# Causal attention on one core: row maxima from K = 32 row strips, two heads per reduction, and four score banks with one exponential for two heads

## The chip, the cores and the metric

The kernel runs on one core of one Trainium2 chip. The metric is the device time of one execution in microseconds (us), and the median of the runs is compared. Three runs of the kernel before gave 3187.44, 3190.36 and 3196.83 us.

## The reference

One transformer layer over T = 2048 tokens with D = 1024 features, in fp32: normalisation, causal attention with 32 query heads of 32 features in 8 groups of 4 (each group shares one key and one value head), an output projection, a second normalisation, and a feed-forward part with int4 weights. Cut to what the change touches:

```
q = (xn @ Wq)  as (32 heads, T, 32);  k, v = (xn @ Wkv) as (8 groups, T, 32) each
scores = q @ k.T                          # causal: key > query is -inf
weights = softmax(scores / sqrt(32))      # exp(s - rowmax) / sum of them
ctx = weights @ v
x = x + layernorm(ctx @ Wo + bo)
x = x + layernorm(ffn(layernorm(x)))
```

## The kernel before, in words

The program is a row of stages, each in its own block: `project_qk`, `attend`, `project_context`, `gate_and_up`, `project_down`. Only `attend` is changed.

`attend` handles the 8 groups one after another. A product in near fp32 is made from fp16 parts: a head's query is stacked in 96 partitions as (high, low, high) and its key as (high, high, low), so one 96-row matmul gives three partial products at once. A 97th row carries the negated row maximum of the query and the constant 256 on the key side, so that the score matmul (`scores`, L464) yields scores from which the maximum is already subtracted, and ScalarE takes the exponential straight from PSUM (L576).

For a group there are 40 steps, (b, k): query block b of 512 queries, key tile k of 128 keys, `k < 4 * (b + 1)`. 28 steps are 512 queries wide; the last three key tiles of each block are 384, 256 and 128 wide, 4 steps each. In each step TensorE makes the scores of four heads (transposed: keys on the partitions), ScalarE takes the exponentials into a ring of five steps (`PROB`), and TensorE multiplies them by the values one step later (`products`, L479, four heads in four 32-column strips of the array, fp32 operands) and by a vector of ones (`sums`, L493), after GpSimd has added two steps' exponentials together where it can (`add_pair`, L695).

The maxima of group g + 1 are found while group g is worked on. `units` lists the pieces: a unit is one head, one tile of 128 queries and up to 1024 keys; there are 96 in a group, handed out over the steps before `TURN` (step 37) by `share` and placed between the scores, products and sums by `cut`. TensorE makes a unit with one or two 96-row matmuls (L445) and, on the diagonal, a masking matmul of 128 columns (L449); VectorE reduces it (L588):

```
S1 = ps("s1", [P, 2, UNIT])          # two slots of two banks: maxima
S2 = ps("s2", [P, 2, BANK])          # two banks: scores, one head each
free = SLOTS * g + (n - 1 if n else 0)   # unit n waits for the reduction of unit n - 2
```

So unit n + 1 is made in the other slot while unit n is reduced. At `TURN` the maxima are transposed (L455), scaled (L600) and stored as row 97 of the query stack by a DMA (L408). Group 0's units come in `ahead`, before the first group, one half of a value tile (12 matmuls of 256 columns, L506 to L508) after every fourth unit.

The order on each engine is fixed by the program; semaphores join the engines. SyncE loads group g + 2 (`load_group`, six DMAs, 1.9 MB, three buffers) at the start of group g. TensorE runs the body of a group as a hardware loop over groups 0 to 6 and a copy of it for group 7 (`bodies`). VectorE has group 0, a loop over 1 to 6, and group 7; ScalarE loops over all 8 groups, GpSimd over 1 to 7.

Of the kernel before, what the change touches and what calls it, by code (L numbers as in the profile page):

```python
# [295 lines left out]
def attend(nc, x_hi, x_lo, wv_hi, wv_lo, qk_hi, qk_lo, v_sb, ident, identb, causal, ones, c_hi, c_lo, sem):  # L296

# [16 lines left out]
    UNIT = 2 * BANK  # L314
    RING = 5
    exp_scale = float(HD) ** -0.5 / MS
    VC = wv_hi.shape[2]

# [3 lines left out]

    assert T == 2 * UNIT
    half = NT // 2
# [3 lines left out]
    EARLY = NT // 4  # L328
    PART = UNITS // (2 * (NT - EARLY))
    SLOTS = UNITS + 1  # L330

    width = [BANK - max(0, k - TPB * b) * P for b, k in steps]
    TURN = STEPS - 3
    share = [min(UNITS, -(-UNITS * sum(width[:s]) // sum(width[:TURN]))) for s in range(STEPS + 1)]
    units_in = [range(share[s], share[s + 1]) for s in range(STEPS)]

# [28 lines left out]
    loaded, max_stored, buffer_free = sem("c_loaded"), sem("c_max_stored"), sem("c_buffer_free")  # L365
# [7 lines left out]


    S2_FREE, PROB_FREE, SUM_FREE, C_FREE, CN_FREE = 2, SUMS, 1, 2, 2

    with ExitStack() as ctx:
        sb = lambda n, s, d=F32: ctx.enter_context(nc.sbuf_tensor("c_" + n, s, d))
        ps = lambda n, s, d=F32: ctx.enter_context(nc.psum_tensor("c_" + n, s, d))
        Q, K = sb("q", [STACK + 1, 3, REP, T], F16), sb("k", [STACK + 1, 3, T], F16)  # L380
        V = sb("v", [P, NT, HD])
        PROB = sb("prob", [P, RING * REP, BANK])
        MAXES, NEGMAX = sb("maxes", [P, NT * REP, 2]), sb("negmax", [P, P])
# [3 lines left out]
        S1 = ps("s1", [P, 2, UNIT])  # L387
        S2 = ps("s2", [P, 2, BANK])
# [6 lines left out]

        @block.sync
        def _(sp):
            def load_group(g, buf):
                qrows, krows = bass.ds(g * P, P), bass.ds(D + g * HD, HD)
                for row, (qs, ks) in enumerate(((qk_hi, qk_hi), (qk_lo, qk_hi), (qk_hi, qk_lo))):  # L400
                    part = slice(row * HD, (row + 1) * HD)
                    sp.dma_start(Q[part, buf], qs[qrows, :].rearrange("(h d) t -> d h t", d=HD)
                                 ).then_inc(loaded, 16)
                    sp.dma_start(K[part, buf], ks[krows, :]).then_inc(loaded, 16)
# [5 lines left out]
            load_group(0, 0)  # L410
            sp.wait_ge(loaded, 96)
            load_group(1, 1)
            store_maxima(0, 0)
            sp.wait_ge(loaded, 192)
            load_group(2, 2)
            store_maxima(1, 1)
            with sp.Fori(1, GROUPS - 2) as g:
                sp.wait_ge(loaded, 96 * g + 192)
                sp.sem_inc(buffer_free, 1)
                sp.wait_ge(scores_done, REP * STEPS * g)  # L420
                sp.sem_inc(buffer_free, 1)
                load_group(g + 2, (g + 2) % 3)
                store_maxima(g + 1, (g + 1) % 3)
            store_maxima(GROUPS - 1, (GROUPS - 1) % 3)

        def bodies(eng, body, ahead):

            ahead()
            with eng.Fori(0, GROUPS - 1) as g:
                body(g, True)  # L430
# [899 lines left out]
```

## Time and profile before

| | |
|---|---|
| median of 3 runs | 3190.36 us (3187.44 to 3196.83) |
| profiled execution, first to last instruction | 3191.3 us |
| `project_qk` | 0 to 256 us |
| `attend`, value tiles and units of group 0 | 256 to 371.2 us |
| `attend`, groups 0 to 6 | 371.2 to 1385.9 us |
| `attend`, group 7 (no units) | 1385.9 to 1507.4 us |
| `project_context` and the stages behind it | 1510 to 3191.3 us |

For the profiled execution no time of its own is listed beside its span; the span lies 0.9 us over the median of the runs. Stage limits are read from the first matmul of a line. In the profile, "busy" of a matmul includes the time in which its last columns leave the array, so that matmuls issued one behind another overlap in the record.

### The profile page before, as it was taken

How to read it: one execution, taken by the hardware profiler on the slowest of the kernel's cores; microseconds unless marked ns; L12 is line 12 of the kernel's file. 1: busy time of each engine (PE TensorE's matmuls, PEld its weight loads, DVE VectorE, ACT ScalarE, POOL GpSimd, SP SyncE). 2: the span in 40 equal slices, each digit the busy share in tenths (PEclk: the TensorE clock that was granted, in tenths of full speed). 3: DMA queues.
4: the chain of work that ended last, by engine and by line, in shares of the span. 5: the costliest groups of instructions: out<-in, count | busy, mean ns of one | idle time of the engine just before them, and what ended most of it. 6: DMA issues, size and time to landing. Idle time of an engine off the chain costs nothing. (4 is left out here: it accounts for less than half of the span.)

```text
span 3191.3 us, 47284 instructions
## 1 busy us (share of the span) xinstructions
PE 2983.2 (93%) x16984; PEld 1287.0 (40%) x16984; DVE 1297.3 (41%) x1707; ACT 946.7 (30%) x1734; POOL 951.0 (30%) x754
## 2 busy tenths in 40 slices
PE   7997798989899899988995999999999999999998
PEld 3444333333333333321443444444444444444443
DVE  5326775756656576620564223322233221000101
ACT  3110255656555565566111111111121111000000
POOL 0000165646455455656112222222222221000101
PEclk9999999999999999999997999999999999999999
DMA  4312101010110100000322111111111110331310
GB/s 157 101 50 60 26 1 27 1 27 1 26 23 5 27 1 2 1 2 14 122 95 70 43 39 43 43 43 39 39 45 44 39 38 24 109 112 62 123 62 26
DMA packets 143507, 144.62 MB, mean 45 GB/s; under 512 B 44272, under 2 KB 120560, under 8 KB 143344
## 3 DMA queue, kind: packets, MB, share of 16 engines
q1 hardware_dynamic: 143344, 142.39, 14.8%
q8 instruction: 110, 1.80, 0.2%
q14 instruction: 53, 0.43, 0.1%
HBM read 92.41 MB, written 49.81 MB: 45 GB/s over the span
## 5 line engine op out<-in xcount | busy, mean ns | idle before, releaser
L588 DVE TENSOR_REDUCE c_maxes<-c_s 128x1 f32<-128x1024 f32 (+7 forms) x768 | 675.0, 905 | 322.5 <-PE c_s L449 172.2
L576 ACT ACTIVATE c_prob<-c_s 128x512 f32<-128x512 f32 (+3 forms) x1280 | 637.8, 532 | 442.2 <-PE c_s L464 243.5
L695 POOL TENSOR_TENSOR c_prob<-c_prob 128x512 f32<-128x512 f32 (+1 forms) x480 | 581.5, 1242 | 431.7 <-ACT c_prob L576 430.2
L464 PE MATMUL c_s<-c_q,c_k 97*128 (+2 forms) x1280 | 415.9, 360 | 77.7 <-ACT c_prob L576 31.1
L445 PE MATMUL c_s<-c_k,c_q 96*128 (+2 forms) x1280 | 371.9, 359 | 34.5 <-DVE c_maxes L588 31.1
L479 PE MATMUL c_ctx<-c_prob,c_v 128*32 128x512 f32 (+3 forms) x2560 | 307.2, 552 | 0.0
L1096 DVE SCALAR_TENSOR_TENSOR e_h<-e_up,e_silu 128x512 f32<-128x512 f32 (+1 forms) x88 | 60.8, 691 | 579.8 <-PE e_up L1058 579.8
L1145 POOL TENSOR_TENSOR e_hl<-e_h,e_hh 128x512 f16<-128x512 f32 (+1 forms) x88 | 101.9, 1158 | 589.0 <-ACT e_hh L1119 589.0
L1056 PE MATMUL e_gp<-x_hi,e_w_hi 128*128 128x512 f16 (+1 forms) x704 | 267.9, 381 | 2.5 <-DVE e_w_lo L1086 2.5
L1057 PE MATMUL e_gp<-x_lo,e_w_hi 128*128 128x512 f16 (+1 forms) x704 | 267.6, 380 | 0.0
L1058 PE MATMUL e_gp<-x_hi,e_w_lo 128*128 128x512 f16 (+1 forms) x704 | 267.6, 380 | 0.0
L1056 PE MATMUL e_up<-x_hi,e_w_hi 128*128 128x512 f16 (+1 forms) x704 | 266.8, 379 | 0.0
L1057 PE MATMUL e_up<-x_lo,e_w_hi 128*128 128x512 f16 (+1 forms) x704 | 266.8, 379 | 0.0
L1058 PE MATMUL e_up<-x_hi,e_w_lo 128*128 128x512 f16 (+1 forms) x704 | 266.8, 379 | 0.0
L464 PEld LDWEIGHTS c_s<-c_q,c_k 97*128 (+1 forms) x1280 | 118.8, 99 | 320.4 <-issue 165.3
L445 PEld LDWEIGHTS c_s<-c_k,c_q 96*128 (+1 forms) x1280 | 103.1, 99 | 324.6 <-DVE c_maxes L588 143.6
L1226 PE MATMUL f_yp<-wd_hi,f_h_hi 128*128 128x512 f16 x704 | 210.4, 381 | 12.1 <-DMA f_h_lo<-h_lo 12.1
L1226 PE MATMUL f_yp<-wd_hi,f_h_lo 128*128 128x512 f16 x704 | 210.3, 380 | 0.0
L1226 PE MATMUL f_yp<-wd_lo,f_h_hi 128*128 128x512 f16 x704 | 210.3, 380 | 0.0
L1119 ACT ACTIVATE e_hh<-e_h 128x512 f16<-128x512 f32 (+1 forms) x88 | 55.4, 630 | 476.5 <-DVE e_h L1096 476.5
L74 DVE BATCH_NORM_STATS2 f_norm_stats<-f_yp 128x6 f32<-128x512 f32 x16 | 11.2, 699 | 424.6 <-PE f_yp L1226 424.6
L1264 POOL TENSOR_TENSOR f_z<-f_x,f_z 128x1024 f32<-128x1024 f32 x16 | 37.2, 2347 | 435.4 <-DVE f_z L87 435.4
(142 smaller groups left out, 3409.2 us busy)
## 6 DMA issues: line engine op xcount, KB each, us to landing
h_hi<-e_hh SPq DMA_DIRECT2D x84, 128.0 KB, 1.8
h_lo<-e_hl SPq DMA_DIRECT2D x84, 128.0 KB, 1.7
f_h_hi<-h_hi SPq DMA_DIRECT2D x7, 1344.0 KB, 8.5
f_h_lo<-h_lo SPq DMA_DIRECT2D x7, 1344.0 KB, 6.9
b_x<-L_attn_x SPq DMA_DIRECT2D x16, 512.0 KB, 6.6
c_q<-qk_hi SPq DMA_DIRECT2D x16, 512.0 KB, 6.6
d_x<-L_attn_x SPq DMA_DIRECT2D x16, 512.0 KB, 5.1
x_dram<-d_x SPq DMA_DIRECT2D x16, 512.0 KB, 2.6
```

What stands on the lines that cost most here:

```text
L445: last = nc.tensor.matmul(S1[:, slot, c:c + n_c], Q[0:STACK, buf, h, t * P:(t + 1) * P], K[0:STACK, buf, u * UNIT + c:u * UNIT + c + n_c], ...
L464: last = nc.tensor.matmul(S2[:, h % 2, j:BANK], K[:, buf, k * P:(k + 1) * P], Q[:, buf, h, b * BANK + j:(b + 1) * BANK], start=True, stop= ...
L479: last = nc.tensor.matmul(CTX[h * HD:(h + 1) * HD, j:BANK], V[:, k, :], PROB[:, REP * (s % RING) + h, j:BANK], start=(k == 0), stop=(k == ...
L576: nc.scalar.activation(PROB[:, REP * (s % RING) + h, j:BANK], S2[:, h % 2, j:BANK], ACT.Exp, scale=exp_scale).then_inc(exp_done, 1)
L588: nc.vector.tensor_reduce(MAXES[:, h * NT + t, u:u + 1], S1[:, n % 2, 0:end], AX.X, ALU.max).then_inc(maxed, 1)
L695: last = nc.gpsimd.tensor_tensor(one, one, two, ALU.add)
L1056: nc.tensor.matmul(o, wh, x2_hi[:, k, tok], start=(k == 0), stop=False)
L1057: nc.tensor.matmul(o, wh, x2_lo[:, k, tok], start=False, stop=False)
L1058: last = nc.tensor.matmul(o, wl, x2_hi[:, k, tok], start=False, stop=(k == KC - 1))
L1096: nc.vector.scalar_tensor_tensor(H[0:n, b % 2, :], UP_[0:n, b % 2, :], HS * in_scale, SILU[0:n, b % 2, :], ALU.mult, ALU.mult).then_inc(h_ ...
L1145: nc.gpsimd.tensor_tensor(HL[0:n, b % 2, :], H[0:n, b % 2, :], HH[0:n, b % 2, :], ALU.subtract).then_inc(lo_done, 1)
L1226: last = nc.tensor.matmul(YP[:, u, s, n:n + BANK], stat, w[:, c, n:n + BANK], start=(c == 0 and a == 1), stop=(c == CHUNKS - 1 and z == 1))
```

## The change

Inside `attend`:

- The maxima come from the high halves alone: `QH` and `KH` hold a group's four query heads in four strips of 32 partitions, and the key's high half four times. A unit is now two heads, one tile of 128 queries and at most 512 keys: two matmuls of 32 rows in two row strips, into the two banks of `S1`, then on the diagonal two masking matmuls of 128 columns, and one reduction of both banks into two columns of `MAXES`. There are 80 units in a group.
- `S1` is one slot: unit n waits for the reduction of unit n - 1.
- `S2` is four banks, one for each head of the group. Scores are made, waited for and exponentiated two heads at a time: 80 exponentials in a group in place of 160, each over two banks.
- Units are matched to steps (`in_step`): one key chunk in both pairs of heads, so two units, in 34 steps; two chunks, so four units, in steps 9, 10 and 11; none from step 37 on.
- The query and key stacks have two buffers. SyncE loads the stack of group g + 1 at the start of group g and the heads of group g + 2 (`load_heads`, five DMAs, 1.0 MB) behind it.
- TensorE, VectorE and SyncE run groups 0 and 1, a loop with two turns over two groups each, and groups 6 and 7 (`all_groups`). The loops of ScalarE and GpSimd stay.
- While group 0's maxima are made, half a value tile stands after each of the first 24 units.

```diff
-    units = [unit for h in range(REP) for a in range(half)
-             for unit in ((h, half + a, 0), (h, a, 0), (h, NT - 1 - a, 1))]
...
+    step_width = [BANK - max(0, k - TPB * b) * P for b, k in steps]
+    PAIR = 2
+    tiles = [(t, u) for t in range(NT) for u in range(t // TPB + 1)]
...
+    def unit_width(tile):
+        t, u = tile[:2]
+        return min(BANK, (t + 1) * P - u * BANK)
...
+    waiting = {w: [tile for tile in tiles if unit_width(tile) == w] for w in range(P, BANK + P, P)}
+    in_step = [[waiting[w].pop(0)] if s < TURN else [] for s, w in enumerate(step_width)]
+    narrow = [s for s in range(TPB, TURN) if step_width[s] < BANK]
+    for w in sorted(waiting, reverse=True):
+        for tile in waiting[w]:
+            in_step[next(s for s in narrow if step_width[s] == w and len(in_step[s]) == 1)].append(tile)
+    in_step = [[(t, u, pair) for pair in range(PAIR) for t, u in row] for row in in_step]
...
-        Q, K = sb("q", [STACK + 1, 3, REP, T], F16), sb("k", [STACK + 1, 3, T], F16)
+        Q, K = sb("q", [STACK + 1, 2, REP, T], F16), sb("k", [STACK + 1, 2, T], F16)
+        QH, KH = sb("qh", [P, 2, T], F16), sb("kh", [P, 2, T], F16)
...
-        S1 = ps("s1", [P, 2, UNIT])
-        S2 = ps("s2", [P, 2, BANK])
+        S1 = ps("s1", [P, PAIR, BANK])
+        S2 = ps("s2", [P, REP, BANK])
...
+        def all_groups(eng, body):
+            for parity in range(2):
+                body(0, parity)
+            with eng.Fori(1, GROUPS // 2 - 1) as i:
+                for parity in range(2):
+                    body(i, parity)
+            for parity in range(2):
+                body(GROUPS // 2 - 1, parity)
...
+            def load_heads(g, buf):
+                sp.dma_start(QH[:, buf, :], qk_hi[bass.ds(g * P, P), :]).then_inc(heads_loaded[buf], 16)
+                for h in range(REP):
+                    sp.dma_start(KH[h * HD:(h + 1) * HD, buf, :], qk_hi[bass.ds(D + g * HD, HD), :]
+                                 ).then_inc(heads_loaded[buf], 16)
...
+            def unit(g, buf, n):
+                t, u, pair = units[n]
+                w = unit_width(units[n])
+                diag = u == t // TPB
+                if not (is_first(g) and n == 0):
+                    pe.wait_ge(maxed, SLOTS * g + n)
+                for h in range(PAIR):
+                    rows = slice((PAIR * pair + h) * HD, (PAIR * pair + h + 1) * HD)
+                    last = nc.tensor.matmul(S1[:, h, 0:w], QH[rows, buf, t * P:(t + 1) * P],
+                                            KH[rows, buf, u * BANK:u * BANK + w], start=True, stop=not diag)
+                if diag:
+                    for h in range(PAIR):
+                        last = nc.tensor.matmul(S1[:, h, w - P:w], identb[:], causal[:], start=False, stop=True)
                 last.then_inc(unit_done, 1)
...
                 for s in range(STEPS):
-                    scores(g, s, (0,))
-                    some_units(s, 0)
-                    scores(g, s, (1,))
+                    ns = list(units_in[s]) if more else []
+                    scores(g, parity, s, 0)
                     if s:
                         products(g, s - 1)
-                    some_units(s, 1)
-                    scores(g, s, (2,))
-                    some_units(s, 2)
-                    scores(g, s, (3,))
+                    for n in ns[:len(ns) // PAIR]:
+                        unit(g + 1, 1 - parity, n)
+                    scores(g, parity, s, 1)
                     sums(g, s)
-                    some_units(s, 3)
+                    for n in ns[len(ns) // PAIR:]:
+                        unit(g + 1, 1 - parity, n)
...
+                    for pair in range(PAIR):
+                        h = PAIR * pair
+                        act.wait_ge(scores_done, PAIR * STEPS * g + PAIR * s + pair + 1)
+                        nc.scalar.activation(PROB[:, REP * (s % RING) + h:REP * (s % RING) + h + PAIR, j:BANK],
+                                             S2[:, h:h + PAIR, j:BANK], ACT.Exp, scale=exp_scale).then_inc(exp_done, 1)
...
                 dve.wait_ge(unit_done, SLOTS * g + n + 1)
-                nc.vector.tensor_reduce(MAXES[:, h * NT + t, u:u + 1], S1[:, n % 2, 0:end],
+                nc.vector.tensor_reduce(MAXES[:, PAIR * pair:PAIR * pair + PAIR, t, u], S1[:, :, 0:unit_width(units[n])],
                                         AX.X, ALU.max).then_inc(maxed, 1)
```

## Rows read from the trace of the kernel before

**Rows 1.** The page: the span, and each engine's busy time.
```profile
span 3191.3 us, 47284 instructions
PE 2983.2 (93%) x16984; PEld 1287.0 (40%) x16984; DVE 1297.3 (41%) x1707; ACT 946.7 (30%) x1734; POOL 951.0 (30%) x754
```

**Rows 2.** Busy time by stretch: group 0's units, group 0, group 6, group 7.
```profile
core 0: us, PE busy (x) PEld busy (x) DVE busy (x) ACT busy (x) POOL busy (x), PEclk, DMA share, GB/s
267.40:371.20 103.80, 72.24 (x514) 44.87 (x515) 83.03 (x98) 5.88 (x13) 0.61 (x1) 0.99 0.10 21
371.20:518.00 146.80, 136.09 (x970) 45.86 (x971) 91.69 (x111) 83.41 (x165) 78.24 (x67) 0.97 0.11 23
1245.80:1385.90 140.10, 135.66 (x969) 45.65 (x969) 92.34 (x113) 81.73 (x164) 79.81 (x68) 0.97 0.01 1
1385.90:1507.40 121.50, 105.54 (x748) 26.69 (x744) 10.05 (x17) 81.22 (x166) 79.05 (x70) 0.96 0.00 1
```

**Rows 3.** Groups of VectorE by form, groups 0 to 7 (371 to 1507 us).
```profile
L588 DVE TENSOR_REDUCE c_maxes<-c_s 128x1 f32<-128x1024 f32 x280 | 339.3, 1218 | 189.2 <-PE c_s L445 137.8 <-PE c_s L449 50.0
...
L588 DVE TENSOR_REDUCE c_maxes<-c_s 128x1 f32<-128x768 f32 x56 | 53.1, 947 | 20.6 <-PE c_s L449 20.6
...
L588 DVE TENSOR_REDUCE c_maxes<-c_s 128x1 f32<-128x512 f32 x56 | 38.0, 679 | 15.9 <-PE c_s L449 15.6
...
L588 DVE TENSOR_REDUCE c_maxes<-c_s 128x1 f32<-128x256 f32 x56 | 23.3, 417 | 10.4 <-PE c_s L449 9.5
L623 DVE STREAM_TRANSPOSE c_st<-c_sum 128x512 f32<-128x512 f32 x32 | 22.7, 709 | 158.4 <-PE c_sum L493 158.4
```

**Rows 4.** Groups of TensorE by form, the same stretch.
```profile
L464 PE MATMUL c_s<-c_q,c_k 97*128 x1120 | 365.2, 359 | 62.4 <-DMA c_k<-qk_hi 29.7 <-ACT c_prob L576 17.9 <-issue 4.1
L445 PE MATMUL c_s<-c_k,c_q 96*128 x1120 | 330.5, 361 | 5.1 <-DVE c_maxes L588 2.6
...
L449 PE MATMUL c_s<-causal,identb 128*128 128x128 bf16 x448 | 100.4, 224 | 0.0
```

**Rows 5.** Timeline of group 6, 1301.3 to 1304 us: start, duration, engine.
```profile
1301.35 0.39 PE L464 MATMUL c_s<-c_q,c_k 97*128 x1 [0.20 <-ACT c_prob L576]
...
1302.01 0.38 PE L464 MATMUL c_s<-c_q,c_k 97*128 x1
...
1302.32 1.06 PE L479 MATMUL c_ctx<-c_prob,c_v 128*32 128x512 f32 x8
...
1303.32 0.50 PE L445 MATMUL c_s<-c_k,c_q 96*128 x2
...
1303.65 0.22 PE L449 MATMUL c_s<-causal,identb 128*128 128x128 bf16 x1
...
1303.91 0.96 DVE L588 TENSOR_REDUCE c_maxes<-c_s 128x1 f32<-128x768 f32 x1 [0.28 <-PE c_s L449]
```

**Rows 6.** Timeline of a group's start, 802.6 to 810.5 us.
```profile
802.50 0.34 SPq L402 DMA_DIRECT2D c_q<-qk_hi  x1
...
803.07 0.60 ACT L567 ACTIVATE c_c<-c_ctx 128x512 f32<-128x512 f32 x1 [0.62 <-PE c_ctx L479]
...
808.15 1.28 ACT L576 ACT_TABLE_LOAD   x1 [4.49 <-issue]
...
809.12 0.59 PE L464 MATMUL c_s<-c_q,c_k 97*128 x1 [5.98 <-DMA c_k<-qk_hi]
...
809.85 0.60 ACT L576 ACTIVATE c_prob<-c_s 128x512 f32<-128x512 f32 x1 [0.41 <-PE c_s L467]
```

**Rows 7.** Busy time in two stretches at a low granted clock (columns as in rows 2).
```profile
806.90:817.10 10.20, 7.95 (x29) 2.71 (x29) 3.93 (x5) 4.65 (x7) 0.00 (x0) 0.50 0.61 125
1711.00:1721.00 10.00, 2.27 (x11) 1.87 (x9) 2.45 (x2) 2.05 (x2) 1.83 (x2) 0.50 0.34 34
```

**Rows 8.** Groups of ScalarE by form, 371 to 1710 us.
```profile
L576 ACT ACTIVATE c_prob<-c_s 128x512 f32<-128x512 f32 x896 | 503.3, 596 | 291.5 <-PE c_s L464 243.5 <-PE c_s L467 34.5
...
L848 ACT ACTIVATE x_hi<-d_xt 128x1024 f32 x14 | 13.6, 1020 | 41.1 <-PE d_xt L789 41.1
```

More of the change, by code:

```diff
@@ L317, in attend @@
     VC = wv_hi.shape[2]
+    assert REP * HD == P and GROUPS % 2 == 0
     steps = [(b, k) for b in range(NB) for k in range(TPB * (b + 1))]
@@ L433, in _ @@
+            all_groups(sp, body)
+            sp.wait_ge(max_stored, 16 * GROUPS)
         @block.tensor
         def _(pe):
-            def unit(g, n):
-                h, t, u = units[n]
-                buf, slot = g % 3, n % 2
-                free = SLOTS * g + (n - 1 if n else 0)
-                if not (isinstance(free, int) and free <= 0):
-                    pe.wait_ge(maxed, free)
-                end = min(UNIT, (t + 1) * P - u * UNIT)
-                for c in range(0, end, BANK):
-                    n_c = min(BANK, end - c)
-                    diag = u * UNIT + c + n_c == (t + 1) * P
-                    last = nc.tensor.matmul(S1[:, slot, c:c + n_c], Q[0:STACK, buf, h, t * P:(t + 1) * P],
-                                            K[0:STACK, buf, u * UNIT + c:u * UNIT + c + n_c],
-                                            start=True, stop=not diag)
-                    if diag:
-                        last = nc.tensor.matmul(S1[:, slot, c + n_c - P:c + n_c], identb[:], causal[:],
-                                                start=False, stop=True)
+            def unit(g, buf, n):
[11 more added lines that the diff above has]
+                        last = nc.tensor.matmul(S1[:, h, w - P:w], identb[:], causal[:], start=False, stop=True)
@@ L525, in body @@
[L525 to L536 removed]
+            pe.sem_inc(sums_done, PROB_FREE)
@@ new lines, in _, with body @@
+            halves = [(i, half) for i in range(NT) for half in range(2)]
+            for _ in range(2 * EARLY):
+                half_value_tile(*halves.pop(0))
+            pe.wait_ge(heads_loaded[0], 80)
+            for n in range(UNITS):
+                unit(0, 0, n)
+                if halves:
+                    half_value_tile(*halves.pop(0))
+            turn_maxima(0)
+            pe.wait_ge(v_done, NT)
+            def body(i, parity):
+                g = 2 * i + parity
+                more = not is_last(g)
+                pe.wait_ge(stack_loaded[parity], 96 * i + 96)
+                pe.wait_ge(max_stored, 16 * g + 16)
+                if more:
+                    pe.wait_ge(heads_loaded[1 - parity], 80 * (i + parity) + 80)
@@ L638, in normalise, with body @@
                 nc.vector.tensor_tensor(CN[:, b % 2, :], C[:, b % 2, :], R[:], ALU.mult).then_inc(normed, 1)
-            def body(g, first_pass, first_group):
-                left = [] if first_group else [(g - 1, NB - 1, i) for i in range(PIECES + 1)]
+            def body(i, parity):
+                g = 2 * i + parity
+                more = not is_last(g)
+                left = [] if is_first(g) else [(g - 1, NB - 1, i) for i in range(PIECES + 1)]
                 def one_piece():
```

150 lines of the change are left out of this document (58 added, 92 removed).

## Prediction

> **What bounds the kernel now.** I began with the page [rows 1]: TensorE is busy in 93% of the span and every other engine in at most 41%. Over a kernel with five stages that says little, so I cut the attention stage by stretch [rows 2]. With units, a group takes 146.8 us (group 0) or 140.1 us (group 6); groups 0 to 5 average (1245.8 - 371.2) / 6 = 145.8. Without units group 7 takes 121.5. Finding one group's maxima alone, before group 0, takes 103.8, with VectorE busy 83.0 of it: that stretch is VectorE's, the groups are TensorE's. The lines confirm it: in the groups L445 waited for VectorE's reductions hardly at all (5.1 us of idle before it), L464 62.4 us, 29.7 of that at group starts [rows 4]. Two slots of maxima are why: VectorE reduces one while TensorE fills the other.
>
> Count TensorE's columns in a group (2.4 GHz, clock near 1.00 in rows 2). The 40 steps hold 17408 columns a head. Scores: 4 x 17408 + 64 masks x 128 = 77824, 32.4 us. Units: the same, 32.4 us. Products: four passes for fp32, four heads side by side: 69632, 29.0 us. Sums: 40448, 16.9 us. Together 110.7 us. The rest of about 137 is changes between full and strip matmuls and waits for exponentials. A 512-wide set of products shows the change: it starts at 1302.32, 0.31 after the scores before it, which stream 0.21; the next matmul starts at 1303.32, 1.00 later, where four passes stream 0.85 [rows 5]. So a set costs 1.09 in place of 0.85, some 0.1 at each change.
>
> A group's start is a place of its own [rows 6]: ScalarE is empty at 803.67, waits 4.49 without a releaser, loads its table (1.28) and is ready at 809.43; TensorE idles 5.98 to 809.12. Both take a loop's back edge there, while SyncE starts its six loads at 802.50. Afterwards the clock stands at half (1.2 GHz) for 10.2 us [rows 7]. Of that I charge 3 us; so a warm group is 140.1 - 3 = 137.
>
> **The change, part by part.**
>
> *Units on TensorE.* Two 32-row matmuls in different strips should stream together, as four 32-column strips already do in the products. The 69632 columns become 34816: 14.5 us a group less. The masks stay at 64 x 128. That is a gain only where TensorE sets the pace.
>
> *One slot.* Unit n now waits for reduction n - 1, so reduction, hand-over, unit and hand-over stand in one line. The parts: a 1024-element reduction 1.22 us [rows 3]; VectorE starts 0.04 after the last matmul's end (1303.65 + 0.22 to 1303.91), and I take 0.06 for the way back; a 512-column matmul after a wait takes 0.39, the second of a pair ending with it [rows 5]. So a full unit costs 1.22 + 0.06 + 0.39 + 0.04 = 1.71. A diagonal one adds a change of mode (0.1) and masks that begin after the pair has streamed: 0.21 + 0.1 + 0.06 + 0.22 = 0.59 in place of 0.39, so 1.91. Those with two rows of 384, 256 and 128 take the reductions of 768, 512 and 256 elements [rows 3]: 0.95, 0.68, 0.42, in all 1.59, 1.26 and 0.95. A group has 48, 8, 8, 8 and 8 of these: 82.1 + 15.3 + 12.7 + 10.1 + 7.6 = 127.8 us, of which the reductions are some 84; before, 96 reductions ran beside the matmuls.
>
> *Where TensorE is longer than this line.* From the second unit of a step to the first of the next it has the unit (0.21), a change (0.1), two scores (0.43) and products (1.09): 1.84, 0.13 over. That is 28 wide steps, 3.6 us; the same with sums in the other half of 12 steps, 1.6; two narrow sums more in three of them, 1.9; narrow steps with wide products, 1.4. Together 8.5. The last three steps have no units, 8.5. VectorE's own pieces (16 a group, transposes 0.71 [rows 3]) mostly fit into the 0.49 in which it waits; 2 show. So a warm group is 127.8 + 8.5 + 8.5 + 2 = 147, against 137: +10 in each of 7 groups, **+70**.
>
> The Trainium skill speaks against the change here ("TensorEngine Tiling (Array Packing)", Performance Considerations, PSUM Bottleneck): tiling speeds up TensorE but not the reading of PSUM, which may become the bottleneck. The reductions keep their 1.22 us, so the trace bears it out; by column counts alone a group would lose 14.5, by the line it gains 10. The same page says that changing the tiling mode drains the engine (Key Properties); the 0.1 at each change agrees.
>
> *Group 0's units.* Nothing else is there to hide the line: 127.8, and 5 more where half a value tile (12 x 0.107 = 1.28, plus changes) outlasts a narrow unit among the first 24. Before, the units took about 100 of the 103.8. That is +33; loads of 1.0 MB first, in place of 1.9, give back 1. For the last 56 units TensorE is busy 0.39 of each 1.71, 23%. A stretch with 2.27 busy of 10 us stayed at half clock [rows 7]; if this one falls to it, each unit takes 0.25 longer, 14 us. I take 5: **+37**.
>
> *Exponentials.* 512 elements take 596 ns, a 1024-element copy out of PSUM 1020 [rows 8]: a pair costs 1.02 in place of 1.19. ScalarE is no bound in groups with units. In group 7 it is part of a loop: a pair's scores, 0.2 of way, its exponential 1.02, products 1.09, the next scores 0.43, about 2.75 for a step without sums, against pairs of steps that now average just under 3 us. Between nothing and the 16 us for which TensorE is idle (121.5 - 105.5 [rows 2]); the loop puts it low: **-6**.
>
> *Group starts.* TensorE has no back edge at six of seven starts, but ScalarE keeps its own: its first exponential comes at 809.43 in place of 809.85, and by then all four scores of the step and some units are issued, which earlier cost about 2 more. Say 2.5 at five starts and less at the two others, with 2.5 given back at TensorE's one remaining edge: **-11**. Ends: nothing, and 7 us at each of 6 (-42) if ScalarE's wait was due to the shared back edge. SyncE's eleven loads hold nothing up: their users come a group later, and maxima are stored at step 37.
>
> Sum: 70 + 37 - 6 - 11 = **+90 us**. The profiled span is 3191.3, 0.9 over the median of 3190.4, so 3190 + 90 = **3280 us**. The stages outside attention stay.
>
> **Bounds.** Down: if strips of rows cost no change of mode, a group loses about 5.5 (-39) and group 0's units 3; with no clock loss, -5; better group starts, -10: about 3223. Up: if the second weight load of a pair isn't hidden (0.1 us; weight loads show about 0.1), 0.1 x 80 x 8 = 64, and 9 if the clock falls: 3353.
>
> **The rivals.**
>
> *The strips don't run together.* The trace shows column strips only. Then each unit takes 0.21 more, 17 us in each of 8 rounds less what TensorE hides: about +115, 3395. For it: no row shows two row strips. Against: the products' four strips. The skill ("TensorE: Matmul & The Clock Gate", Part 3) gives 3.07 times for four row strips, which would leave the forecast as it is.
>
> *TensorE was the bound and stays it (faster).* If reducing two rows of 512 with the hand-overs takes clearly less than 1.71, the line drops under TensorE's own work: 96.2 us of columns plus about six changes a step, 24, and waits, some 127 a group. That is -10 x 7, +15 for group 0's units, -6 and -11: -72, 3118. It decides from the point where a unit costs 90 / (80 x 8) = 0.14 us less than I reckon; at that point the time is unchanged. For it: 14.5 us of columns really go, and L464's waits do. Against: reductions of 1024 took 1218 ns on average over 280 of them [rows 3], and nothing in two rows shortens the reading.
>
> *Nothing moves.* The unit costs 0.12 to 0.16 us less, or group starts lose nearly all of their 9 us beside cheap changes of mode: within 10 us of 3190.
>
> **Chances.** Forecast, one line of maxima bounds the groups, 3223 to 3353: 0.70. Strips apart, about 3395: 0.10. Slower by less than in the forecast's range, 3200 to 3223: 0.05. Unchanged: 0.05. Faster: 0.10. The range 3205 to 3375 takes in the forecast's bounds and the small loss, and leaves out some 2 in 10 or a little more: faster, unchanged, and most of the strips apart. About 0.3% (10 us) is what a measurement of this kernel can tell from no change: faster 0.10, same 0.05, slower 0.85.
>
> **What would show it.** In the profile after: L588's successor in two forms of about 1.22 us, 56 a group, VectorE idle about 0.5 before nearly each, released by the unit's matmul, and TensorE idle before the units, released by VectorE; group 6 at about 150; group 0's units about 137 from first to last scores; two unit matmuls starting within 0.01. Wrong in its size, if the two start 0.21 apart, or the unit stretch stands at clock 0.5. Wrong in its mechanism, if VectorE isn't what the units wait for, or if group 7 falls under 105. The step I trust least is the change of mode around row strips; next the group starts.

## The result and the profile after

The changed kernel takes 3305.47 us (median of 4 runs, 3304.09 to 3312.01) against 3189.28 for the kernel before on the same chip (4 runs, 3187.44 to 3196.83). The ratio is 1.036, with a 95% interval of 1.035 to 1.038: 116 us slower, where 90 were forecast. The profiled spans differ by 3303.7 - 3191.3 = 112.4, and the accounts below are made in spans.

Page of the kernel after: span, busy time of each engine, granted clock in 40 slices.

```profile
span 3303.7 us, 43445 instructions
PE 2969.6 (90%) x16984; PEld 1227.2 (37%) x16984; DVE 1305.5 (40%) x1579; ACT 877.6 (27%) x1094; POOL 948.7 (29%) x754
PEclk9998579898988898999999799999999999999999
```

No engine's busy time grew by more than 8.2 us (VectorE, 1297.3 to 1305.5) [rows 1]. Of 112 us longer, the page shows little but a lower clock in the early slices. Cut by stretch, the difference is: the first stretch (group 0's units) 148.6 us in place of 103.8 and begun 1.4 later, +46.2; groups 0 to 6, from 417.4 to 1507.1, 1089.7 in place of 1014.7, +75.0; group 7, from the start of the first score to the start of the last exponential, 108.7 in place of 119.9, -11.2; everything behind it +2.4. Together 112.4.

Busy time by stretch after, columns as in [rows 2]: the first stretch, its last 102 us, a whole group, the last group with units, group 7.

```profile
268.80:417.40 148.60, 78.61 (x514) 38.18 (x514) 85.97 (x82) 6.27 (x14) 0.61 (x1) 0.66 0.04 9
315.40:417.40 102.00, 34.23 (x131) 7.09 (x131) 60.07 (x55) 0.00 (x0) 0.00 (x0) 0.50 0.01 1
727.60:879.50 151.90, 130.85 (x973) 37.30 (x970) 93.98 (x98) 74.61 (x86) 80.08 (x69) 0.94 0.09 21
1353.70:1507.10 153.40, 132.38 (x973) 37.77 (x969) 93.98 (x98) 74.64 (x85) 80.08 (x69) 0.93 0.06 14
1507.10:1615.80 108.70, 93.90 (x728) 26.03 (x728) 9.50 (x16) 72.20 (x85) 78.41 (x69) 1.00 0.00 1
```

In a group both engines have idle time now: TensorE 21 us of 151.9 (group 2), VectorE 58. That is the mark of a line in which each waits for the other. VectorE's groups by form in the eight groups say the same; beside each is the idle time before it and its releaser.

```profile
L593 DVE TENSOR_REDUCE c_maxes<-c_s 128x2 f32<-128x1024 f32 x392 | 480.6, 1226 | 247.6 <-PE c_s L462 192.8 <-PE c_s L466 53.9
L593 DVE TENSOR_REDUCE c_maxes<-c_s 128x2 f32<-128x768 f32 x56 | 53.7, 959 | 46.0 <-PE c_s L466 46.0
L593 DVE TENSOR_REDUCE c_maxes<-c_s 128x2 f32<-128x512 f32 x56 | 38.8, 693 | 57.5 <-PE c_s L466 57.5
L593 DVE TENSOR_REDUCE c_maxes<-c_s 128x2 f32<-128x256 f32 x56 | 23.8, 426 | 35.0 <-PE c_s L466 35.0
```

Of the first form there are 392 / 7 = 56 a group, as forecast; two rows of 512 take what one row of 1024 took (1226 against 1218 ns). The idle time before a reduction is 0.63 us on average, released by TensorE. On TensorE's side, the table of waits for the same stretch (engine, tile, line, releaser: us, times, longest):

```profile
PEld c_s L462 <- DVE c_maxes L593: 463.8, 515, 1.3
PE c_s L462 <- DVE c_maxes L593: 139.1, 194, 1.1
```

The line itself is in the timeline of group 2 (weight loads and other engines left out):

```profile
792.83 0.39 PE L462 MATMUL c_s<-c_kh,c_qh 32*128 32x512 f16 x2
...
793.15 0.60 PE L478 MATMUL c_s<-c_q,c_k 97*128 97x512 f16 x2
...
793.25 1.23 DVE L593 TENSOR_REDUCE c_maxes<-c_s 128x2 f32<-128x1024 f32 x1
...
794.54 0.39 PE L462 MATMUL c_s<-c_kh,c_qh 32*128 32x512 f16 x2 [0.79 <-DVE c_maxes L593]
...
794.97 1.23 DVE L593 TENSOR_REDUCE c_maxes<-c_s 128x2 f32<-128x1024 f32 x1 [0.49 <-PE c_s L462]
...
795.39 1.06 PE L493 MATMUL c_ctx<-c_prob,c_v 128*32 128x512 f32 x8
...
796.39 0.39 PE L462 MATMUL c_s<-c_kh,c_qh 32*128 32x512 f16 x2
```

Read three things. The pair of row-strip matmuls is over in 0.39, as long as one matmul after a wait, and in every unit of this trace the second starts 3 or 4 ns after the first: the strips stream together. From unit to unit, where the line binds, it is 794.54 - 792.83 = 1.71 us, the forecast figure: 1.23 of reduction, 0.06 of way back, 0.42 from the unit's start to the next reduction. And from there to the next unit, with products (1.06) between them, it is 796.39 - 794.54 = 1.85: there TensorE is the longer one, by the 0.13 forecast. What the line costs shows against reductions that find their next unit ready: in the kernel before, with two slots, the commonest step from one reduction's start to the next is 1.14 us.

A group's start, 726.9 to 731 us, where ScalarE still turns its loop:

```profile
727.56 0.60 ACT L573 ACTIVATE c_c<-c_ctx 128x512 f32<-128x512 f32 x1 [0.62 <-PE c_ctx L493]
...
727.57 0.39 PE L478 MATMUL c_s<-c_q,c_k 97*128 97x512 f16 x1
...
728.18 1.28 ACT L582 ACT_TABLE_LOAD   x1
...
729.47 1.94 ACT L582 ACTIVATE c_prob<-c_s 128x1024 f32<-128x1024 f32 x2
```

Against [rows 6]: the table load follows the copy after 0.02 us in place of 4.49, and TensorE does not idle at all in place of 5.98. Only where TensorE's own loop turns, at 1039.2, does it idle 6.28 us.

What was won there is lost in the middle of the group. A stretch before the clock falls, and the stretch at half clock, with four units in each of steps 9, 10 and 11:

```profile
757.00:766.00 9.00, 6.28 (x56) 2.16 (x48) 5.50 (x6) 3.02 (x4) 6.97 (x8) 1.00 0.01 2
765.90:783.00 17.10, 14.38 (x86) 4.63 (x86) 5.89 (x10) 4.01 (x7) 1.19 (x2) 0.50 0.00 1
```

Steps 9 to 12 take 27.5 us in group 6; at full clock they would take about 20.8 by an estimate. Step 9 took 6.75 in group 2, where the clock held to its end; step 11 took 4.53 in two groups where the clock was back for half of it; step 12 would take 3.71 as step 24 does; for step 10 no run of this kernel has a full-clock figure, and 5.8 stands between the 5.36 that it takes with a shorter reduction (experiment 6) and the 6.4 with the difference of four reductions added. So the half clock costs 6 to 7 us, 6.7 in what follows, in every group with units (17 to 24 us at half clock). Before, a group had one such stretch of 10.2 us, behind its start [rows 7].

### The profile page after: what moved, and what is told of

It is laid out like the page before. It is cut to its first block and busy times, and to the rows that moved or that the text cites. A ratio compares the mean times of both kernels' runs of the same rounds, so it can differ in the third digit from the quotient of the medians.

```text
span 3303.7 us, 43445 instructions
## 1 busy us (share of the span) xinstructions
PE 2969.6 (90%) x16984; PEld 1227.2 (37%) x16984; DVE 1305.5 (40%) x1579; ACT 877.6 (27%) x1094; POOL 948.7 (29%) x754
## 5 line engine op out<-in xcount | busy, mean ns | idle before, releaser
L593 DVE TENSOR_REDUCE c_maxes<-c_s 128x2 f32<-128x1024 f32 (+3 forms) x640 | 682.3, 1066 | 453.8 <-PE c_s L466 227.1
L582 ACT ACTIVATE c_prob<-c_s 128x1024 f32<-128x1024 f32 (+3 forms) x640 | 568.7, 895 | 704.7 <-PE c_s L481 401.1
L462 PE MATMUL c_s<-c_kh,c_qh 32*128 32x512 f16 (+3 forms) x1280 | 247.6, 383 | 205.6 <-DVE c_maxes L593 204.5
L478 PE MATMUL c_s<-c_q,c_k 97*128 97x512 f16 (+3 forms) x1280 | 375.0, 366 | 10.7 <-issue 9.0
L462 PEld LDWEIGHTS c_s<-c_kh,c_qh 32*128 32x128 f16 x1280 | 61.2, 92 | 583.7 <-DVE c_maxes L593 557.2
L74 DVE BATCH_NORM_STATS2 f_norm_stats<-f_yp 128x6 f32<-128x512 f32 x16 | 11.2, 700 | 425.1 <-PE f_yp L1224 425.1
L507 PE MATMUL c_sum<-c_prob,ones 128*32 128x512 f32 (+3 forms) x1600 | 178.2, 550 | 0.1
```

Source lines behind the costliest of these rows:

```text
L462: last = nc.tensor.matmul(S1[:, h, 0:w], QH[rows, buf, t * P:(t + 1) * P], KH[rows, buf, u * BANK:u * BANK + w], start=True, stop=not diag)
L478: last = nc.tensor.matmul(S2[:, h, j:BANK], K[:, buf, k * P:(k + 1) * P], Q[:, buf, h, b * BANK + j:(b + 1) * BANK], start=True, stop=not ...
L507: last = nc.tensor.matmul(SUM[h * HD:(h + 1) * HD, j:BANK], ones[:], PROB[:, REP * (s % RING) + h, j:BANK], start=(n == first_sum[b]), sto ...
L582: nc.scalar.activation(PROB[:, REP * (s % RING) + h:REP * (s % RING) + h + PAIR, j:BANK], S2[:, h:h + PAIR, j:BANK], ACT.Exp, scale=exp_sc ...
L593: nc.vector.tensor_reduce(MAXES[:, PAIR * pair:PAIR * pair + PAIR, t, u], S1[:, :, 0:unit_width(units[n])], AX.X, ALU.max).then_inc(maxed, 1)
```

## The experiments

Ratios are against the kernel before on the same chip, whose medians lie between 3187.05 and 3190.05. Differences in us from the changed kernel, or between two experiments, can be between chips. Times of stretches and steps are of the profiled execution.

**1. strips_two_slots.** The strips stay; the maxima get two slots, the scores two banks and one exponential each, as before. With the scores made head by head again, the units of a step also stand in up to four places among them, not in two, so this is more than a change of slots.

```diff
-        S1 = ps("s1", [P, PAIR, BANK])
-        S2 = ps("s2", [P, REP, BANK])
+        S1 = ps("s1", [P, 2, PAIR, BANK])
+        S2 = ps("s2", [P, 2, BANK])
...
-                if not (is_first(g) and n == 0):
-                    pe.wait_ge(maxed, SLOTS * g + n)
+                slot = n % 2
+                if not (is_first(g) and n < 2):
+                    pe.wait_ge(maxed, SLOTS * g + (n - 1 if n else 0))
```

> The maxima in row strips, two heads to a unit, but in two slots of two banks; the scores go back to two banks and one exponential per head. Theory (the single slot, one line of reduction, hand-over and unit, is what costs): the line is gone, units run beside reductions again. A wide step without sums falls from 3.57 us to about 3.0, a group from about 153 to 133 to 138, the first group's units from 148.6 to about 105 to 115; 3305 becomes about 3160, faster than the 3190 of the kernel before. Rival (the row strips themselves cost, in changes of mode or because they make VectorE's reads slower): a group stays at 145 or more and the time over 3190.

3179.38 us, ratio 0.998 (0.997 to 0.999): 126 us under the changed kernel. The first stretch takes 104.4 us, groups 137 to 150, a wide step without sums 3.04 us in place of 3.57. The loss goes with the single slot; experiments 6 and 11 change less and say the same. But the starts of groups are long again, though TensorE turns its loop at only one of them:

```profile
657.94 1.28 ACT L588 ACT_TABLE_LOAD   x1 [3.58 <-issue]
...
659.89 0.61 PE L478 MATMUL c_s<-c_q,c_k 97*128 97x512 f16 x1 [4.86 <-ACT c_prob L588]
```

**2. spread_tiles.** The three extra tiles go to wide steps 17, 25 and 33 in place of the narrow steps 9 to 11, so that the line's waits are not bunched.

```diff
-            in_step[next(s for s in narrow if step_width[s] == w and len(in_step[s]) == 1)].append(tile)
+            in_step[{3 * P: 17, 2 * P: 25, P: 33}[w]].append(tile)
```

> The changed kernel with the three extra tiles of steps 9, 10 and 11 (two units more each) moved to the wide steps 17, 25 and 33. Theory (the clock falls to half in steps 9 to 12 because TensorE mostly waits for reductions there): the 20.5 us at half clock go away in groups 1 to 6, steps 9 to 12 lose about 7 us of 27.5 beside the moved work, in all 35 to 50 us: about 3260. Rival (the clock falls for the work of the group's start or for something that does not hang on these steps): the half clock stays and the time stays within 5 us of 3305.

3312.33 us, 1.039 (1.037 to 1.041): no gain. The half clock moved with the tiles: in group 2 it stands for 6.8 us at step 17 and for 3.4 each at steps 25 and 33, 13.6 in all, where the changed kernel has 17 to 24. The stretch at step 17:

```profile
793.00:799.80 6.80, 6.29 (x26) 1.08 (x26) 2.64 (x3) 2.05 (x2) 4.25 (x4) 0.50 0.00 0
```

Step 17, now with four units, takes 7.18 us in place of 3.57. Steps 18, 26 and 34, with two units each as before, take 6.31, 4.89 and 5.24 in place of 3.71, 3.57 and 3.71, so 5.5 us of loss lie there at half clock. A group still takes 153.6 us: a third less time at half clock brought nothing. The dips follow the steps in which TensorE waits through four units, and are not a thing of that part of a group.

**3. spread_values.** In the first stretch, half a value tile stands after every third unit to the end, not after each of the first 24, to keep TensorE busy throughout.

```diff
-                if halves:
+                if halves and n % 3 == 2:
```

> The changed kernel with half a value tile after every third unit of the first group in place of every one of the first 24. Theory (the clock falls in the first group's units because TensorE is busy for under a third of the time once the value tiles are through): the 102 us at half clock shrink to the last units, each unit loses 0.25 us, and the value tiles hide in the wait for the reductions: the stretch falls from 148.6 to about 130, the kernel to about 3287. Rival (the value tiles cost the same wherever they stand and the clock is no matter): within 4 us of 3305.

3329.1 us, 1.045 (1.042 to 1.047), worse by 24; the theory that this would keep the clock up fell. The stretch takes 174.8 us at a mean clock of 0.63:

```profile
268.20:443.00 174.80, 105.70 (x515) 50.25 (x515) 86.01 (x82) 6.28 (x14) 0.61 (x1) 0.63 0.04 9
```

```profile
331.42 0.61 PE L462 MATMUL c_s<-c_kh,c_qh 32*128 32x512 f16 x2
...
332.07 1.23 DVE L593 TENSOR_REDUCE c_maxes<-c_s 128x2 f32<-128x1024 f32 x1 [2.68 <-PE c_s L462]
...
333.35 0.39 PE L462 MATMUL c_s<-c_kh,c_qh 32*128 32x512 f16 x2 [1.32 <-DVE c_maxes L593]
```

At half clock a half value tile is 12 x 256 columns, by count 2.56 us, twice the reduction beside which it should hide; VectorE waits 2.68 for the unit behind it. Why the clock falls more often here than with the tiles in a row is not shown.

**4. before_straight_pe.** The kernel before, with TensorE's groups written out in place of its loop; every other engine keeps its own.

```diff
-            with eng.Fori(0, GROUPS - 1) as g:
-                body(g, True)
-            body(GROUPS - 1, False)
+            for g in range(GROUPS):
+                body(g, g < GROUPS - 1)
```

> The kernel before, with the groups of TensorE's program written out in a row in place of a loop; the other engines keep their loops. Theory (the wait of 5.6 to 6.4 us at a group's start is the way back of TensorE's loop, and the half clock behind it follows from it): TensorE's idle time there goes, the clock stays up, 9 us a start, some 45 in all: about 3145. Rival (ScalarE's own loop, which waited 4.5 us there, sets the start): ScalarE's wait stays, TensorE then waits for ScalarE, and no more than 10 us are gained: 3180 or more.

3172.33 us, 0.995 (0.993 to 0.996): 15 us won. TensorE's own wait is gone. ScalarE's stays, 3.9 to 4.6 us at five starts and 2.1 at the last two, and TensorE waits for it:

```profile
661.17 1.28 ACT L575 ACT_TABLE_LOAD   x1 [4.13 <-issue]
...
663.12 0.61 PE L463 MATMUL c_s<-c_q,c_k 97*128 97x512 f16 x1 [5.40 <-ACT c_prob L575]
```

ScalarE's wait does not come from TensorE turning its loop at the same time.

**5. one_strip.** In the changed kernel both matmuls of a pair use the same strip of 32 rows.

```diff
-                    rows = slice((PAIR * pair + h) * HD, (PAIR * pair + h + 1) * HD)
+                    rows = slice(PAIR * pair * HD, (PAIR * pair + 1) * HD)
```

> The changed kernel, with both matmuls of a unit in the row strip of the pair's first head (the second head's maxima are then those of the first, so the output changes). Theory (unit and reduction stand in one line, and the two strips run together): the pair now streams one after the other, 0.21 us more on the line in each 512-wide unit, about 0.19 on average, 14 us a group and 15 in the first stretch: 3305 becomes 3400 to 3430. Rival (the strips do not run together in the changed kernel either): no change, 3305.

3520.36 us, but its four runs lie from 3475.83 to 3588.01, and no interval is given. All lie over the 3400 to 3430 expected. The timeline is clear all the same: the pair takes 0.60 (the second matmul starts 0.23 after the first), and VectorE waits 0.84 where it waited 0.49.

```profile
899.71 1.23 DVE L593 TENSOR_REDUCE c_maxes<-c_s 128x2 f32<-128x1024 f32 x1 [0.84 <-PE c_s L462]
...
901.13 0.60 PE L462 MATMUL c_s<-c_kh,c_qh 32*128 32x512 f16 x2
...
901.77 1.23 DVE L593 TENSOR_REDUCE c_maxes<-c_s 128x2 f32<-128x1024 f32 x1 [0.84 <-PE c_s L462]
```

A wide step goes from 3.57 to 3.99 us: +0.42, two units by 0.21. What TensorE adds to a unit is paid in full, so the changed kernel's strips do run together, and the line binds. Group 1 takes 170.1 us in place of 153.6, near the 14 expected; other groups take up to 202.4 at a clock of 0.75, and the first stretch 172.9, so the rest of the excess goes with time at half clock.

**6. half_reduction.** The changed kernel reduces only the first half of each unit's columns.

```diff
-                nc.vector.tensor_reduce(MAXES[...], S1[:, :, 0:unit_width(units[n])],
+                nc.vector.tensor_reduce(MAXES[...], S1[:, :, 0:unit_width(units[n]) // 2],
```

> The changed kernel, reducing only the first half of a unit's columns (so the maxima, and the output, are of half the keys). Theory (the reduction is on the line that sets the groups): a 512-wide unit's line falls from 1.71 to about 1.18 us, until TensorE's own work sets the pace at about 133 us a warm group in place of 146; the first stretch falls from 148.6 to about 110, the half clock in steps 9 to 12 gets shorter: 3150 to 3190, at or under the kernel before. Rival (TensorE's changes of mode around the strips set the pace): under 30 us gained.

3180.47 us, 0.996 (0.995 to 0.998): 125 us under the changed kernel. The first stretch falls to 121.9 us, a wide step without sums to 3.03; one with sums stays at 3.71. Groups 1 and 2, the first at full clock, TensorE busy in 93% of it:

```profile
531.70:666.50 134.80, 125.24 (x973) 36.20 (x969) 60.51 (x98) 74.71 (x86) 80.27 (x69) 1.00 0.10 23
666.50:804.40 137.90, 128.34 (x974) 36.61 (x970) 60.47 (x98) 74.71 (x86) 80.28 (x69) 0.98 0.10 23
```

So with a shorter reduction the line no longer sets the wide steps. The half clock stays in all groups but this one: groups 2 to 6 take 137.9 to 150.2 us, with 7 to 31 us of it. In group 2 steps 9 to 11, the ones with four units, take the same 5.55, 5.36 and 3.68 us as in group 1, and only there does the clock fall behind them.

**7. before_one_slot.** The kernel before, with its 96 units of one head, in one slot.

```diff
-                buf, slot = g % 3, n % 2
-                free = SLOTS * g + (n - 1 if n else 0)
+                buf, slot = g % 3, 0
+                free = SLOTS * g + n
```

> The kernel before, with all its 96-row units in the first of its two slots, nothing else changed. Theory (the slot alone is what costs): 96 units in line, each about 0.9 us of reduction and 0.5 to 0.75 of hand-overs and matmuls; a group rises from 137 warm to about 165 to 175 and the first stretch from 104 to about 150: 3430 to 3500. Rival (TensorE sets the groups in any case): under 3250.

3643.69 us, 1.143 (1.141 to 1.146), above what either theory gave. Its first stretch and a group:

```profile
270.10:473.20 203.10, 126.38 (x515) 61.70 (x513) 88.23 (x98) 6.27 (x14) 0.61 (x1) 0.63 0.05 10
...
861.10:1060.50 199.40, 152.50 (x970) 45.15 (x971) 97.84 (x114) 84.94 (x166) 79.78 (x69) 0.90 0.06 13
```

The units of 1024 keys put two matmuls one behind another into the line, there are 96 units, and the clock is lower in both stretches than in the changed kernel; how the excess is shared among these was not measured. It shows that the slot's loss needs nothing of the strips.

**8. one_exp_per_head.** The changed kernel with its four score banks, but one exponential for each head: 160 in ScalarE's loop body in place of 80.

```diff
-                    for pair in range(PAIR):
-                        h = PAIR * pair
-                        act.wait_ge(scores_done, PAIR * STEPS * g + PAIR * s + pair + 1)
+                    for h in range(REP):
+                        act.wait_ge(scores_done, REP * STEPS * g + REP * s + h + 1)
```

> The changed kernel with one exponential per head again, 160 a group, still over four banks. Theory (ScalarE is no bound with units; what the pairing brought is ScalarE's way back at a group's start, whose loop body has half as many instructions): groups with units stay at about 146 warm, ScalarE's wait of 4 to 4.6 us comes back at the starts and costs 4 to 7 us in each of 6 or 7 groups, group 7 rises from 108.6 towards 115 to 118: 3305 becomes 3330 to 3360. Rival (the wait at the start went because TensorE's loop went): the starts stay free, only group 7 changes: 3305 to 3315.

3351.27 us, 1.051 (1.049 to 1.053): 46 us over the changed kernel. Steps are the same (3.57 and 3.71 us), and group 7 takes 108.8: the expected rise there did not come. The difference is at the starts, where ScalarE waits 3.9 to 5.2 us again at six of them, and 2.06 at group 7's:

```profile
739.85 1.28 ACT L581 ACT_TABLE_LOAD   x1 [3.90 <-issue]
...
742.28 0.50 PE L478 MATMUL c_s<-c_q,c_k 97*128 97x384 f16 x1 [3.73 <-ACT c_prob L581]
```

**9 and 10. two_slots_straight and before_straight_pe_act.** Experiments 1 and 4, with ScalarE's groups written out too. In the first this leaves only GpSimd's loop; in the second VectorE and SyncE keep theirs as well.

```diff
-            with act.Fori(0, GROUPS) as g:
+            for g in range(GROUPS):
                 for s in range(STEPS):
```

> The strips with two slots, with the groups written out in a row on TensorE, VectorE, SyncE and ScalarE (no loop is left but GpSimd's). Theory (ScalarE's wait of about 4 us at a start is the way back of a loop whose body is long): the wait goes at all seven starts, with TensorE's 7 us at the one start where its loop turned; steps 0 and 1 of a group fall from about 13.5 to about 6.5 us: 3179 becomes about 3125. Rival (the wait is the fetch of instructions while eleven loads run, whatever the loop): it stays at the starts where loads run, and under 15 us are gained.

> The kernel before, with TensorE's and ScalarE's groups written out in a row. Theory (as for the version with two slots): ScalarE's wait goes too, about 5 us a start beside the version with TensorE alone, 3172 becomes about 3138; strips in two slots are then worth the difference to that version, about 3 us in each of 7 groups, some 10 to 20 us. Rival (strips in two slots bring nothing): the two end within 5 us of each other.

Strips in two slots: 3115.25 us, 0.977 (0.976 to 0.979). The kernel before: 3124.45 us, 0.980 (0.979 to 0.981), where 3138 was expected. The two are 9 us apart, against 10 to 20 expected. A group of each, in this order:

```profile
785.60:919.40 133.80, 131.99 (x973) 38.92 (x969) 94.62 (x98) 84.50 (x165) 80.30 (x69) 1.00 0.10 24
```

```profile
782.80:918.00 135.20, 131.64 (x974) 44.83 (x971) 92.76 (x114) 81.50 (x165) 80.39 (x69) 1.00 0.07 16
```

Clock 1.00 and TensorE busy in 97% or more of the group, in both. ScalarE's wait at the starts is gone, and so is its table load of 1.28 us there; SyncE's loads still run at these starts, so they alone do not make the wait. With the starts out of the way, strips in two slots save 1.4 us a group; the 14.5 us of columns that they remove do not show as time. No run separates what takes their place; changes between full and strip matmuls would be the first to look at.

**11. first_group_two_slots.** The changed kernel, but group 0's units use the banks of the scores, idle then, as a second slot.

```diff
+                to = S2[:, PAIR:, :] if ahead and n % 2 else S1
...
-                    pe.wait_ge(maxed, SLOTS * g + n)
+                    pe.wait_ge(maxed, SLOTS * g + n - ahead)
```

> The changed kernel, where group 0's units alternate between the two banks of the maxima and banks 2 and 3 of the scores, which nothing uses by then; all other groups keep one slot. Theory (the first stretch is the same line of reduction and unit, and no work hides it): it falls from 148.6 to about 100 to 108, where VectorE's 84 us of reductions set it, and 3305 becomes about 3262. Rival (the half clock there, not the slot, made the loss): under 20 us gained.

3261.18 us, 1.023 (1.022 to 1.025): the first stretch is back at 104.7 us, though the clock falls to half at 312.4 and stays there to its end. The whole stretch, and ten us in its second part:

```profile
266.90:371.60 104.70, 77.64 (x515) 38.14 (x515) 81.53 (x82) 6.28 (x14) 0.61 (x1) 0.72 0.08 18
...
340.00:350.00 10.00, 5.27 (x20) 0.92 (x18) 10.00 (x10) 0.00 (x0) 0.00 (x0) 0.50 0.00 0
```

At half clock VectorE is busy without a gap and starts a reduction every 1.13 us, much as at full clock in experiment 12, where full-width units follow each other in 1.13 to 1.18. In the changed kernel a unit of this stretch takes 1.93 at half clock in place of 1.71. So half clock costs nothing where TensorE works beside VectorE; it costs 0.22 a unit where it stands in line with it.

**12. two_slots_best.** Experiment 9 with the value halves of experiment 3.

> The version with two slots and the groups in a row, with half a value tile after every third unit of group 0 in place of every one of the first 24. With one slot the same edit cost 24 us. Theory (there a value tile at half clock outlasted the reduction it stood behind, in line; with two slots TensorE is busy enough for the clock to stay up, and the tiles lie beside reductions): the half clock from 316 to 398 us goes, the first stretch falls from 104.3 to about 100, group 0 from 143.9 to about 138, 3115 becomes about 3106. Rival (spreading the tiles costs whatever the slots): the first stretch grows to over 115 us and the time to over 3122.

3106.75 us (3104.9 to 3107.16), 0.974 (0.973 to 0.975), the fastest of all and the time expected. With a slot to spare the same spreading that lost 24 us in experiment 3 now wins 8: the first stretch takes 93.8 us in place of 104.3, with 9 of them at half clock, and group 0 takes 137.4 in place of 143.9.

```profile
270.90:364.70 93.80, 66.58 (x515) 37.36 (x514) 80.89 (x82) 4.98 (x13) 0.61 (x1) 0.95 0.06 14
```

## Why the prediction was right, and where its sizes were off

The direction, the mechanism and the range held; the sum was 22 us short of the profiled difference. By its terms:

*One slot in the groups, +70: right in its working, measured about +80.* The line of 1.71, and TensorE's 0.13 on top where products lie between, are in the timeline to 0.01. A group at full clock would take 153.4 - 6.7 = 146.7 us (147 forecast). The reference was off: the kernel before, without its starts, takes 135.2 (experiment 10), not 137. So the line costs 11.5 x 7 = 80.5, and experiments 1, 6 and 9 show whose it is: with a second slot or half a reduction a wide step falls from 3.57 to 3.04. Against strips in two slots, the single slot costs 146.7 - 133.8 = 12.9 us a group. All of these carry the 0.5 by which the 6.7 may be off. The Trainium skill's warning ("TensorEngine Tiling (Array Packing)", Performance Considerations, PSUM Bottleneck) is borne out here: 1226 ns for two rows of 512 against 1218 for one of 1024.

*Group 0's units, +37: too small, measured +44.8, and 1.4 of later start.* The step that failed is "I take 5" of a possible 14 for the clock. The stretch fell to half at 315.4 us and stayed there to its end, with TensorE busy 34.23 of 102 us. A pair takes 0.61 at half clock in place of 0.39, so some 54 units pay about 0.22 each, 12 us, of which the prediction took 5. Experiment 11 shows that the slot makes the clock matter: with two slots the reductions follow each other as fast at half clock as at full.

*Group starts, -11: wrong, about -52.* The failed step is "ScalarE keeps its own back-edge wait". It was taken for a property of the loop, and of the stated ends the far one (-42) had the wrong condition. Experiment 4 refutes a shared back edge: the wait stays without TensorE's loop. Experiment 8 shows what it hangs on: the changed kernel with 160 exponentials in ScalarE's loop body has it, with 80 it does not. In sum: before, seven groups took 68.3 us more than 7 x 135.2. After, they take 62.8 more than 7 x 146.7, of which 7 x 6.7 = 46.9 are the half clock in the middle. That leaves 15.9 for starts, nearly all of it at the one turn of TensorE's loop: 6.28 idle, and about 8 in a longer stretch at half clock behind it. The prediction also had SyncE's loads hold nothing up; the last paragraph of this section has rows against that.

*Half clock inside the groups: not foreseen, +47.* The prediction had it only at starts and in the first stretch. It follows the steps with four units (experiment 2), in which TensorE waits through four turns of the line; but experiment 6 has groups with such steps and both outcomes, so what tips the clock is not settled. This and the better starts nearly cancel: -5.5 in place of -11. That the sum of the two was nearly right is luck: two errors of over 40 us each.

*Exponentials, -6: measured -11.2*, inside the range of 0 to 16. An exponential of a pair takes 1023 ns (1.02 forecast). Experiment 8 kept the gain with single exponentials (108.8), so it comes from the four banks, not from the joined exponential. Experiments 9 and 10, with two banks and no loop on TensorE or ScalarE, take 113.5 for this group, and experiment 4, where of these two only ScalarE keeps its loop, 118.3: of the 11 us some 1.6 lie with TensorE's loop, 4.8 in ScalarE's turn and 4.8 in the banks. The parts don't add up cleanly, since experiment 8 turns ScalarE's loop before group 7 too (a wait of 2.06 us only) and loses nothing there.

*Stages outside: 0, measured +2.4.*

The rivals: strips that don't run together are ruled out (the pair in 0.39 against 0.60 in experiment 5). TensorE as the bound is what experiment 6 makes: a reduction takes 0.69 in place of 1.23, far past the 0.14 at which the prediction set the decision, and the time falls by 125 us. But it ends only 9 us under the kernel before, not 72: the rival counted some 127 us a group for TensorE's own work, and experiments 6 and 9 have groups of 134.8 and 133.8 at full clock. Of the signs named beforehand, the 56 reductions, VectorE's 0.49 before them, their releaser, the pair that streams together and group 7 over 105 came; group 6 took 153.4 rather than 150, group 0's units 148.6 rather than 137, and their stretch stood at clock 0.5, the sign named for "wrong in its size".

Open after these runs: why ScalarE waits some 4 us at the turn of a loop of 160 exponentials and not of one of 80. The traces say where that time goes. In the kernel before, the wait from 803.67 to 808.15 holds this:

```profile
q1 hardware_dynamic: 261, 0.94, 99.2%
...
q14 instruction: 1, 0.01, 1.0%
```

These are the packets of two DMA queues in 803.7 to 808.2: SyncE's loads, and one packet of 8 KB of a queue that the profile calls "instruction". In the five versions that loop over 160 exponentials, each of ScalarE's 35 waits at the start of groups 1 to 7 has such a packet in it (twice two). The six versions with 80 in the loop and the three without a loop have no such wait at any of 63 starts, though packets of this queue land at other times. TensorE's 20 idle times of 3.6 us or more at the starts of groups 1 to 7 have at least one packet of 16 KB of a second instruction queue in them. The waits are longer where loads run. Where SyncE loads nothing, at the last one or two starts, the packet begins 0.4 to 0.7 us after the engine falls idle and ScalarE waits 2.05 to 2.45; where loads run, it begins 1.4 to 2.8 us after, and the wait is 3.6 to 5.7. So at its turn the engine seems to wait for instructions that come by DMA, behind the loads. That the packet ends the wait is inferred from its place in time: no run moved the loads away from a turn, and the size of body at which the wait begins, between 80 and 160 exponentials, was not measured.

## What to carry to other kernels

A buffer pair in PSUM is worth what runs beside it: with one slot, every part of producer, reducer and both hand-overs is paid in full (1.71 us a unit here, where reductions alone follow each other in 1.13), and the engine's clock, harmless off the path, becomes part of the price. Cutting columns on the busiest engine brought 1.4 us of 14.5 a group; writing out the loops brought 65 us to the kernel before (3189 to 3124). Before crediting a rearrangement of work, look at the gaps where loops turn, on each engine, ask which of them the change touches by its count of instructions alone, and look at what the DMA queues carry in them.

## What was unexpected of the hardware

- ScalarE's wait at its loop's turn: with 160 exponentials in the body 3.6 to 5.7 us while loads run and 2.05 to 2.45 without, 0.02 with 80. TensorE idles 5.6 to 7.2 us at a turn while loads run (3.71 once, in experiment 7), 3.7 and 4.1 without, and none where the groups are written out.
- TensorE's clock was at half (1.2 GHz) after stretches in which the engine had still worked much: 6.28 of 9.00 us busy before one of the falls, and it stayed there in a stretch with 34.23 of 102 busy. At full clock it stayed through a group with 125.24 busy of 134.8, and fell in the next group of the same run, with the same steps before.
- Two 32-row matmuls in different row strips, each into its own bank, end together: 0.39 for the pair and 0.60 in one strip. Diagonal units pay for both masks one behind another: below, at half clock, the pair (0.40), two masks (0.39) and a reduction of two rows of 256 stand in one line, 1.51 us from unit to unit.

```profile
766.29 0.40 PE L462 MATMUL c_s<-c_kh,c_qh 32*128 32x256 f16 x2
...
766.61 0.39 PE L466 MATMUL c_s<-causal,identb 128*128 128x128 bf16 x2
...
767.04 0.69 DVE L593 TENSOR_REDUCE c_maxes<-c_s 128x2 f32<-128x512 f32 x1 [0.96 <-PE c_s L466]
...
767.80 0.39 PE L462 MATMUL c_s<-c_kh,c_qh 32*128 32x256 f16 x2 [0.79 <-DVE c_maxes L593]
```
